# GINE layers of a graph network: the clear on GpSimd taken out, a limit of three groups put in

## What is computed

```python
src, dst = (edge_index[0], edge_index[1])
for l in range(3):
    e = edge_attr @ W_lin[l] + b_lin[l]          # 50000 x 32 by 32 x 128
    msg = relu(x[src] + e)                       # a gather of 50000 rows of 128 floats
    agg = segment_sum(msg, dst, num_segments=n)
    h = x + agg
    h = relu(h @ W1[l] + b1[l]) @ W2[l] + b2[l]
    h = batch_norm(h, gamma[l], beta[l])
    x = relu(h)
```

## Time and profile before

| what | us |
|---|---|
| median of three runs | 4524.12 |
| the profiled execution | 4522.14 |
| its span, first to last instruction | 4520.3 |
| the three GINE layers in it, first gather of the first to last gather of the last | 1654.4 to 3449.0 |
| GpSimd busy, whole span | 2825.8 |
| mean granted clock of TensorE | 0.797 of full speed |

### The profile page before, as it was taken

One profiled execution on the slowest core, in us unless ns is written; L12 is line 12 of the kernel. 1 busy time (PEld: TensorE's weight loads), 2 busy tenths in 40 slices (PEclk: granted clock), 3 DMA queues, 4 the chain that ended last, 5 costly groups with the idle time before them and its releaser, 6 DMA issues. The chain is left out here.

```text
span 4520.3 us, 91957 instructions
## 1 busy us (share of the span) xinstructions
PE 3424.3 (76%) x20700; PEld 2666.3 (59%) x20793; DVE 2652.9 (59%) x6184; ACT 1615.5 (36%) x3137; POOL 2825.8 (63%) x2944
## 2 busy tenths in 40 slices
PE   6999999967777755555655555555556799999997
PEld 3777777745555534444444444444444688898894
DVE  5888888866666653333333333333334788888885
ACT  3666666645555531111211111211113333333334
POOL 4555555537777758888678888588884444444440
PEclk7999999979999965555555555655556899999998
DMA  3333333313223212222122222122221333333330
GB/s 113 92 100 100 99 99 100 101 48 80 80 80 80 79 50 59 58 58 59 47 68 59 58 59 59 55 60 58 59 59 48 108 110 110 106 110 109 106 101 15
DMA packets 293253, 349.80 MB, mean 77 GB/s; under 512 B 63537, under 2 KB 236756, under 8 KB 292916
## 3 DMA queue, kind: packets, MB, share of 16 engines
q0 software_dynamic: 98528, 229.12, 17.9%
q1 hardware_dynamic: 140481, 92.05, 7.5%
q10 hardware_dynamic: 54162, 27.77, 2.2%
HBM read 332.61 MB, written 16.07 MB: 77 GB/s over the span
## 5 line engine op out<-in xcount | busy, mean ns | idle before, releaser
L988 POOL DMA_INDIRECT gath<-source_rows_narrow,gine_idx x1176 | 1136.7, 967 | 386.2 <-issue 316.1
L1038 DVE TENSOR_TENSOR vs<-psum,gath 128x512 f32<-128x512 f32 x366 | 253.1, 692 | 1027.7 <-SPq L973 954.0
L1004 PE MATMUL psum<-gine_lin,ea 32*128 32x128 f32 x2928 | 288.4, 483 | 749.3 <-DVE vs L1038 721.7
L1144 POOL DMA_INDIRECT gath<-source_rows,idx_all x416 | 430.3, 1034 | 509.5 <-DVE vs L1265 352.8
L760 POOL DMA_INDIRECT gath<-source_rows,idx_all x488 | 465.1, 953 | 377.2 <-PE psum L807 262.3
L1004 PEld LDWEIGHTS psum<-gine_lin,ea 32*128 32x128 f32 x2928 | 183.8, 297 | 849.9 <-DVE vs L1038 778.7
L760 POOL DMA_INDIRECT gath<-source_rows_narrow,idx_all x488 | 462.8, 948 | 206.1 <-issue 136.6
L790 PE MATMUL psum<-lk,att_b 128*128 128x512 f32 x732 | 375.2, 619 | 113.8 <-DVE lk L885 113.2
L1068 ACT ACTIVATE pm<-vs 128x512 f32<-128x512 f32 x186 | 117.2, 630 | 811.1 <-DVE vs L1038 806.6
L807 PEld LDWEIGHTS psum<-gath,pt 128*128 128x128 f32 x2928 | 365.1, 192 | 36.8 <-DVE zsum L918 1.8
L1013 PE MATMUL psum<-hot,pm 128*128 128x128 f32 x1488 | 363.4, 421 | 20.4 <-ACT pm L1068 19.4
(11 more groups left out here) (243 smaller groups left out, 6412.2 us busy)
## 6 DMA issues: line engine op xcount, KB each, us to landing
rel<-rel_rows SPq DMA_DIRECT2D x244, 128.0 KB
ea<-in_edge_attr_tiles SPq DMA_DIRECT2D x416, 64.0 KB
ea<-in_edge_attr ACTq DMA_DIRECT2D x366, 64.0 KB
gath<-source_rows_narrow,gine_idx POOLq DMA_INDIRECT x1176
gath<-source_rows,idx_all POOLq DMA_INDIRECT x904
rel<-quad_rel_rows SPq DMA_DIRECT2D x104, 128.0 KB
gath<-source_rows_narrow,idx_all POOLq DMA_INDIRECT x488
source_rows<-ACC SPq DMA_DIRECT2D x12, 512.0 KB, 2.9
```

Source lines behind the costliest of these rows:

```text
L988: pool.indirect_dma_start(out=ring[:, g % RING, j, :], out_offset=None, in_=table1, in_offset=bass.IndirectOffsetOnAxis(ap=gine_idx[:, g, ...
L1004: last = e.matmul(E[:, j, :], ea[rows, s, :], gine_lin[rows, layer, :], start=True, stop=True)
L1038: v.tensor_tensor(vs[:, s, :].rearrange("p (j d) -> p j d", j=SUBS), E, ring[:, bass.ds(slot, 1), :, :].rearrange("p a j d -> p (a j) d"), ...
L1144: pool.indirect_dma_start(out=gath[:, q % 4, j, :], out_offset=None, in_=table, in_offset=bass.IndirectOffsetOnAxis(ap=quad_idx[:, q, j:j ...
```

## The change

The clear and its semaphore go away. GpSimd waits, before the gathers of group g, for group g-3 to be used, in place of g-8 (the ring keeps its eight slots). SyncE reports group g-1 as used after the landing of group g, in place of g-4, and at the end of a layer one group in place of four.

```diff
 RING = 8
+AHEAD = 3
...
-        gi_landed, gi_free, gi_paused = sem("gine_landed"), sem("gine_free"), sem("gine_paused")
+        gi_landed, gi_free = sem("gine_landed"), sem("gine_free")
...
                         sp.nop().then_inc(gi_landed, 1)
-                        if not isinstance(g, int) or g >= 4:
-                            used(g - 4)
+                        if not isinstance(g, int) or g >= 1:
+                            used(g - 1)
 
                     by_group(sp, group)
-                    for g in range(GROUPS - 4, GROUPS):
-                        used(g)
+                    used(GROUPS - 1)
...
                     for g in range(GROUPS):
-                        if g >= RING:
-                            pool.wait_ge(gi_free, layer * GROUPS + g - RING + 1)
+                        if g >= AHEAD:
+                            pool.wait_ge(gi_free, layer * GROUPS + g - AHEAD + 1)
                         for j in range(SUBS):
                             pool.indirect_dma_start(
                                 out=ring[:, g % RING, j, :], out_offset=None, in_=table1,
                                 in_offset=bass.IndirectOffsetOnAxis(ap=gine_idx[:, g, j:j + 1], axis=0)).then_inc(gi_gath[g % RING], 16)
-                        wait(pool, gi_paused, layer * GROUPS + g)
-                        pool.memset(hot_t[0:1, :, :], 0.0).then_inc(gi_paused, 1)
```

## The result

The changed kernel takes 4297.36 us (median of four runs, 4296.32 to 4298.96), the kernel before 4526.49 (four runs, 4523.55 to 4529.8): a ratio of 0.9497, with a 95% interval of 0.9482 to 0.9511, 229 us less. Forecast were 4282 and 242 less. The profiled execution of the changed kernel took 4298.28, its span 4296.5; against the profiled execution of before that is 223.9 less.

What follows compares the result with a forecast made beforehand. GpSimd's nonstop gathers were taken to bound the GINE stage. 4522.1 - 254.1 (all steps at 1.252 us) + 12 (new loss) = 4280.0, and 2.0 for the median gave 4282 us, ratio 0.946; 8-in-10 range 4260 to 4345.

Steps and rivals of the forecast that it cites:

- GpSimd's pace bounds the stage, and the clear lies on it: GINE stage: GpSimd gathers without a stop; removing 291 clears between gathers saves 0.79 us each, 229.9 us.
- today's loss of 24.2: Time the kernel before loses in gathers prolonged beyond 0.947 us, 94 of them longer than 1 us: 24.2 us.
- A step without a clear is 1.252 us: Time from one gather's start to the next on GpSimd, read from the second GAT stage: 1.252 us.
- The new wait is met: GpSimd's wait on SyncE's report of group g-3 doesn't bind: 2.66 us to spare, cost taken as 0.
- the chain's 2.65 us: SyncE's report comes 2.65 us after a group's gathers: 1.78 of landing plus 0.87 of SyncE's work.
- Rivals 2 and 3: 2: landing grows, GpSimd's new wait binds, slower, chance 0.04; 3: clear's time returns in gaps or gathers, 4524 us, 0.03.
- The third gather leads the compare: After the change a group's third gather starts 0.10 us ahead of VectorE's compare; some 14 would be held up.
- the new loss, 12 us: Gathers prolonged by VectorE's compares after the change: 9 us from offsets, taken as 12 for shifted successors.
- this too ends before the next group lands: Two-block groups: adds 2.83 us apart, said to finish before the next group's gathered rows land.
- 0.51 us less the gather's delay: What one gather loses when it starts after VectorE's compare: 0.51 us minus how far behind it starts.
- The bound beside it: Upper bound on the new gather loss, one hit in every group: 294 x 0.50 = 147 us.
- the forecast's own 4268 to 4305: The main forecast's own range of times, for a gather loss of 0 to 35 us; chance 0.74.

Runs made afterwards that it cites:

- e1: The kernel before with only the clear and its wait taken out, limits and reports as they were: 4296.38 us, ratio 0.9495.
- e9: The kernel before, clear and limits kept, with the compare's row of 0 to 127 read from PSUM: 4494.82 us, ratio 0.993.
- e6: The changed kernel with the compare's row of 0 to 127 copied once per layer into a PSUM bank and read there: 4265.57 us, ratio 0.9422.
- e2: The kernel before with the limit of three groups and the report one group behind, clear left in: 4527.29 us, ratio 0.9998.
- e3: The changed kernel with a limit of two groups in place of three: 4951.64 us, ratio 1.094.
- e5: The changed kernel with the one-hot compare moved right behind the add, ahead of the sum: 4339.12 us, ratio 0.9582.
- e8: The changed kernel with the sum always into block 0, so VectorE loads no block number: 4375.22 us, ratio 0.9669.
- e7: The changed kernel with only two of the four sub-tiles summed, half of those matmuls left out: 4294.44 us, ratio 0.9489.
- e4: The changed kernel with the one-hot compare moved behind the landing wait, ahead of the add: 4286.26 us, ratio 0.9471.

## Why the prediction was right, and where it was off

- **GpSimd's pace bounds the stage, and the clear lies on it.** Shown, by e1 and by e9 less e6: 229 us. That is all of the gain. The forecast had some 12 us more, since it took today's loss of 24.2 away and put 12 in its place. By the medians the collisions cost 31.5 us before (e9) and 31.8 in the changed kernel (e6): the change moved them and took none away.
- **A step without a clear is 1.252 us.** 1.249 in e6. Rows of another stage with the same form of gather gave it to within 0.3%.
- **The new wait is met.** Shown by e2 (no cost) and e3 (the chain's 2.65 us was 2.57). Rivals 2 and 3 didn't come: nowhere in the changed kernel does SyncE release a gather, and the landing is at 1.83 us (median) against 1.79 before.
- **The third gather leads the compare.** It did, by more than forecast: 5 third gathers held up in place of 14, with the landing 0.04 later than in the trace of before. Denser issue isn't shown to be the cause of that: with the clear in, the one-block groups' add is at 1.84 us in e2 and at 1.83 in e9. How thin the lead is, e5 and e8 show.
- **The term that was mis-sized: the new loss, 12 us, measured 30.3.** The step that failed is the sentence on a two-block group's two adds, "this too ends before the next group lands". The adds do end before, at 5.45 us after the group's last gather, but that wasn't enough: VectorE can start its next add only 2.8 to 2.9 us behind the second one, at some 7.6, where the next landing is at 6.8. I had taken the 2.83 us between two adds as TensorE's and had counted no such spacing behind the second block. It is VectorE's sequencer that sets it (e7, e8, and its steps laid end to end). With the clear in, a group took 5.80 us and the next landing, at 7.6, hid this. Shorter groups uncovered it, and brought these compares to the fourth gather. That is 21.9 of the 30.3 us.
- **The cost of one collision was a little short.** The prediction has "0.51 us less the gather's delay"; its own rows, 0.09 us of delay and 0.47 of loss, give 0.56, and so do all traces. For its 39 collisions that is 2 us more. The same slip is in the expectation of e5. And 0.69 in place of 0.51 for 39 collisions is 7 us, not 5.
- **The bound beside it held, the range with some luck.** No run comes near 147 us of loss; the worst, e8, has 103.5. 4297 lies in 4260 to 4345, and in the forecast's own 4268 to 4305 as well. But that own range allowed for a loss of 0 to 35 us without saying from what, and the 21.9 us at the fourth gathers, which the prediction hadn't seen coming, just fitted into it.

## What to carry to other kernels

If an engine runs without a stop and sets a stage's pace, anything on it that isn't needed is paid nearly in full (the clear took 0.94 us and cost 0.79, as the gap behind it was 0.16 in place of 0.30), and what the next engine reports can be checked beforehand by its distance in microseconds from where it is wanted. When a cycle gets shorter, work out again for every kind of item, the rare ones too, where each instruction of the other engines now falls; an overlap that cost nothing in the old cycle may not be free in the new one. Where two instructions collide over an operand, try first to take the operand elsewhere, and only then to move one of them: here moving gave 11 us at best (e4) and cost 42 at worst (e5), and e8, which moved it unawares, cost 78, where the operand in PSUM gave all of the 32.

## What the runs showed of the hardware

- An indirect gather that starts some 0.04 to 0.55 us behind VectorE's compare, which has two SBUF operands, is prolonged by 0.56 us less that delay, to 1.466 us at most in place of 0.947, though the compare runs for 0.69. One that starts ahead of the compare, or less than 0.038 us behind it, isn't prolonged. The rule in the Trainium skill, "SBUF — State Buffer", section "SBUF: two separate sides", by which whoever starts first has the port for the whole instruction, would allow 0.69 less the delay.
- On VectorE the loading of a number from SBUF into a register takes 0.30 us, of two 0.53 us, and these loads with their register steps, not the instructions that compute, set 2.8 to 2.9 us per item where no landing is awaited. Without the load of one number and its steps it is 2.02 (e8).
- An indirect gather of 128 rows costs GpSimd 0.945 us and 0.30 to the next, and a clear of 1 x 1024 bf16 0.94 us, as much as a gather.
